# First feed-forward step of batches 1 to 7 fed from a transposed copy of x, with its LayerNorm applied behind the product

## The reference

```
x = x + 0.5 * ffn(layernorm(x))
x = x + attention(layernorm(x))          # 16 query heads, 4 key heads, head size 128,
                                         # rotary positions, causal window of 64
x = x + 0.5 * ffn(layernorm(x))
ffn(z) = (layernorm(z) * gamma + beta) @ ternary(weight).T + bias
```

## Time and profile before

| | us |
|---|---|
| median of 3 runs | 801.95 (799.03 to 803.97) |
| profiled execution, its own time | 804.61 |
| its span, first to last instruction | 802.8 |
| PE busy | 786.4 (98%) |
| DVE busy | 643.8 (80%) |
| ACT busy | 509.1 (63%) |
| POOL busy | 452.8 (56%) |

### The profile page before, as it was taken

One profiled execution on the slowest core, in us unless ns is written; L12 is line 12 of the kernel. 1 busy time (PEld: TensorE's weight loads), 2 busy tenths in 40 slices (PEclk: granted clock), 3 DMA queues, 4 the chain that ended last, 5 costly groups with the idle time before them and its releaser, 6 DMA issues. The chain is left out here.

```text
span 802.8 us, 16164 instructions
## 1 busy us (share of the span) xinstructions
PE 786.4 (98%) x5688; PEld 735.5 (92%) x5688; DVE 643.8 (80%) x1310; ACT 509.1 (63%) x1623; POOL 452.8 (56%) x440
## 2 busy tenths in 40 slices
PE   7899999999999999999999999999999999999997
PEld 6699999999999999999999999999999999999896
DVE  7788868978788887888779887797778888787666
ACT  4277665676656665676657766567665676665583
POOL 4767726575465645656545664456645574564533
PEclk9999999999999999999999999999999999999998
DMA  8462324341352423333233332434225341333500
GB/s 298 113 167 54 93 48 103 99 108 41 66 130 69 106 53 91 92 82 93 53 93 93 77 93 47 103 93 108 51 53 124 87 106 41 82 77 67 132 1 27
DMA packets 52447, 70.53 MB, mean 88 GB/s; under 512 B 7056, under 2 KB 30096, under 8 KB 52368
## 3 DMA queue, kind: packets, MB, share of 16 engines
q1 hardware_dynamic: 51808, 69.17, 35.4%
q10 hardware_dynamic: 560, 0.34, 0.1%
HBM read 10.76 MB, written 4.19 MB: 19 GB/s over the span
## 5 line engine op out<-in xcount | busy, mean ns | idle before, releaser
L1140 POOL TENSOR_TENSOR probs<-probs,inv_sum 128x512 f32<-128x512 f32 x128 | 133.2, 1041 | 186.6 <-DVE inv_sum L828 186.4
L1028 ACT ACTIVATE probs<-scores_p,neg_max 128x128 f32<-128x128 f32 x512 | 181.1, 373 | 50.7 <-DVE neg_max L822 50.2
L609 PE MATMUL attn_p<-wo_s,headsT 128*128 128x256 f32 x1536 | 209.8, 286 | 0.3 <-ACT headsT L1050 0.3
L609 PE MATMUL job_p<-xnT,wq_s 128*128 128x512 f32 x768 | 205.1, 403 | 0.8 <-DVE lnT L887 0.4
L609 PEld LDWEIGHTS attn_p<-wo_s,headsT 128*128 128x128 f32 x1536 | 197.1, 192 | 5.1 <-ACT headsT L1050 0.6
L1151 POOL TENSOR_TENSOR q_s<-q_s,rope_swap 128x512 f32<-128x512 f32 x128 | 164.7, 1294 | 52.1 <-DMA rope_swap<-rope_sin 51.8
L1050 ACT ACTIVATE headsT<-heads_p,columns_s 128x512 fp32r<-128x512 f32 x128 | 88.3, 690 | 146.7 <-PE heads_p L609 145.3
L609 PEld LDWEIGHTS job_p<-xnT,wq_s 128*128 128x128 f32 x768 | 136.0, 189 | 25.6 <-DVE k_s L867 1.1
L625 PE MATMUL scores_p<-k_s,q_s 128*128 128x128 f32 x1024 | 135.3, 275 | 2.0 <-POOL q_s L1151 2.0
L856 DVE SCALAR_TENSOR_TENSOR rope_sin<-job_p,columns_s,rope_t 128x512 f32<-128x512 f32 x160 | 119.1, 744 | 14.2 <-PE job_p L609 13.5
L625 PEld LDWEIGHTS scores_p<-k_s,q_s 128*128 128x128 f32 x1024 | 126.1, 192 | 3.9 <-POOL q_s L1151 2.2
(11 more groups left out here) (80 smaller groups left out, 974.1 us busy)
## 6 DMA issues: line engine op xcount, KB each, us to landing
rope_swap<-rope_sin SPq DMA_DIRECT2D x320, 128.0 KB, 2.3
v_odd<-v_s SPq DMA_DIRECT2D x64, 192.0 KB, 3.3
x_in<-x SPq DMA_DIRECT2D x15, 256.0 KB, 3.3
out<-x_res SPq DMA_DIRECT2D x15, 256.0 KB, 2.5
q_s<-wq SPq DMA_DIRECT2D x3, 512.0 KB, 10.2
q_s<-wo SPq DMA_DIRECT2D x2, 512.0 KB, 10.3
x_res<-wo SPq DMA_DIRECT2D x2, 512.0 KB, 4.2
x_res<-wv SPq DMA_DIRECT2D x1, 512.0 KB, 7.6
```

What stands on the lines that cost most here:

```text
L609: mm = nc.tensor.matmul(dst, a(p), b(q), start=clears and i == 0, stop=len(pairs) == 1, skip_group_check=True)
L1028: ins = nc.scalar.activation(probs[:, i, k, :], scores_p[i][:, k, :], ACT.Exp, bias=neg_max[:, i, k:k + 1], accum_out=row_sum[:, i, k:k + 1])
L1140: nc.gpsimd.tensor_tensor(probs[:, i, :, :], probs[:, i, :, :], inv_sum[:, i, :].unsqueeze(2).to_broadcast([P, 4, P]), ALU.mult).then_inc( ...
```

## The change

The host passes a second copy of x, transposed in each batch (x_transposed). For batches 1 to 7, load0 brings it into x_tr (512 KB, a third transfer behind the two of x_in), all on SP. YT no longer is a step of PE for these batches, and norm0/norm1 go from ACT: ACT and DVE make lnT straight from x_tr, without mean and rstd. FO multiplies as before. Behind it DVE computes rstd * product + x_in, one instruction of 128x256 for each block. What the mean contributes is -mean * rstd * (gamma summed through W), a row vector gamma_w: POOL's new step offset writes it for a half (128x512, over the part of x_tr that was read), and its new step center adds it to x_in; FO's addition waits for center. Gamma is halved once (gamma0i, POOL, first in its prologue, waits for the columns' transfer), so the factor 0.5 goes from FO's addition. gsum0i (PE, four matmuls, and a copy by DVE) makes gamma_w in the prologue. The mask is kept as two blocks and broadcast. Batch 0 and the second feed-forward steps keep their YT.

All tables are laid anew. What is spoken of below: load0n stands first in the middle list of SP, before the swap of K1c (it stood behind Q6c's); in the last list of SP, shift1c and store1p stand before Q10c, and store0p before K3c, where both stores stood between K3c, Q12c and Q14c; in the last list of TENSOR, FO0c stands behind O15c and YT2c (it stood before O15c); in its middle list, Q6c stands before T0c.

```diff
@@ TENSOR "middle"
-        K1c Q4c O13p W14p S0c T15p S1c Q5c V10c O14p W15p T0c Q6c S2c
...
-        W4c T5c YT0n S7c K3c O4c W5c T6c S8c Q12c YT1n O5c W6c Q13c
+        K1c O13p W14p Q4c S0c T15p S1c Q5c V10c O14p W15p Q6c T0c S2c
...
+        W4c T5c S7c K3c Q12c O4c W5c T6c S8c O5c Q13c W6c T7c S9c
@@ TENSOR "last"
-        T14c YT0c O13c W14c T15c O14c W15c FO0c O15c YT2c FO2c YT3c FO3c
+        YT0c T14c O13c W14c T15c O14c W15c O15c YT2c FO0c FO2c YT3c FO3c
@@ GPSIMD
-        scale0n scale1n half0i bias0n bias1n ascale0n ascale1n w6i w3i w1i w8i K0n Q0n Q1n
+        gamma0i scale0n scale1n half0i bias0n bias1n ascale0n ascale1n w6i w3i w1i w8i K0n Q0n
...
-        K1c Q4c probs0c scale0p probs1c Q5c bias0p Q6c probs2c scale1p Q7c K2c probs3c bias1p
-        Q8c probs4c scale0n probs5c Q9c Q10c probs6c bias0n scale1n Q11c bias1n K3c probs7c residual0c
+        K1c Q4c scale0p probs0c Q5c probs1c bias0p Q6c probs2c scale1p Q7c K2c probs3c bias1p
+        scale0n bias0n probs4c probs5c Q8c Q9c Q10c Q11c scale1n probs6c bias1n offset0n center0n probs7c
+        residual0c offset1n probs8c center1n ascale0n probs9c ascale1n K3c Q12c Q13c Q14c probs10c Q15c probs11c
@@ SYNC "middle" and "last"
-        K1c Q4c Q5c Q6c load0n Q7c K2c Q8c Q9c Q10c store0p store1p Q11c K3c
+        load0n K1c Q4c Q5c Q6c Q7c K2c Q8c Q9c Q10c shift1c Q11c store0p store1p
...
-        K1c Q4c Q5c Q6c Q7c K2c Q8c Q9c Q10c Q11c K3c shift1c store1p Q12c
-        Q13c store0p Q14c Q15c store2c store0c store3c
+        K1c Q4c Q5c Q6c Q7c K2c Q8c Q9c shift1c store1p Q10c Q11c store0p K3c
+        Q12c Q13c Q14c Q15c store2c store0c store3c
@@
+def from_x(x):
+    return x[0][-1] == "1" and x[2] > 0
...
+                sp.dma_start(x_tr[:, :, :], x_transposed[b].rearrange("(c p) t -> p c t", p=P)).then_inc(xt_loaded, 16)
...
+            def gamma_product(_):
+                for e in range(EC):
+                    mm = nc.tensor.matmul(attn_p[1][:, 0, :], gamma_s[:, e:e + 1].to_broadcast([P, P]),
+                                          w_tern[:, e, :].bitcast(F32), start=e == 0, stop=e == EC - 1)
...
@@ ffn_in_low (DVE, L887)
-                        out=lnT[:, r, 1, e, 0:width], in0=bank[:, e * width:(e + 1) * width],
+                        out=lnT[:, r, 1, e, 0:width], in0=transposed_part(x, e), scalar=gamma_s[:, e:e + 1], in1=lnT[:, r, 0, e, 0:width].bitcast(F32), op0=ALU.mult,
...
@@ ffn_out (DVE, L902), for batches 1 to 7
+                        ins = nc.vector.scalar_tensor_tensor(out=dst[:, at, :], in0=bank[:, k, :], scalar=rstd[:, at:at + 1],
+                                                             in1=src[:, at, :], op0=ALU.mult, op1=ALU.add)
...
@@ POOL
+            def mean_offset(x):
+                nc.gpsimd.tensor_tensor(scratch_of(m), gamma_w[:, :].unsqueeze(1).to_broadcast([P, 2, E]),
+                                        shift[:, half].unsqueeze(2).to_broadcast([P, 2, E]),
+                                        ALU.mult).then_inc(offset_ready, 1)
+            def center(x):
+                nc.gpsimd.tensor_tensor(x_in[:, half, :], x_in[:, half, :], scratch_of(m), ALU.add).then_inc(centered, 1)
+            def halve_gamma(_):
+                pool.wait_ge(columns_in, 16)
+                nc.gpsimd.tensor_scalar(gamma_s, gamma_s, 0.5, None, ALU.mult).then_inc(gamma_ready, 1)
```

More of the change, by code:

```diff
@@ L59 @@
     "prologue": """
-        fill0i total0i fill1i YT0n YT1n fill2i beta0i FO0n fill3i FO1n open0i fill4i XT0n fill5i
-        XT1n V00n K0n Q0n Q1n Q2n Q3n V01n
+        fill0i total0i fill1i YT0n YT1n fill2i beta0i FO0n fill3i FO1n open0i gsum0i fill4i XT0n
+        fill5i XT1n V00n K0n Q0n Q1n Q2n Q3n V01n
     """,
     "first": """
-        K1c Q4c Q5c S0c S1c Q6c V10c T0c Q7c S2c W0c T1c S3c K2c
-        O0c W1c T2c Q8c S4c Q9c V11c O1c W2c T3c Q10c O2c W3c S5c
-        T4c S6c Q11c O3c W4c T5c YT0n S7c K3c O4c W5c Q12c O5c T6c
@@ L67 @@
[L67 to L70, removed]
+        K1c Q4c Q5c S0c S1c Q6c V10c T0c S2c Q7c W0c T1c K2c O0c
+        S3c Q8c W1c T2c Q9c V11c S4c O1c W2c T3c Q10c O2c W3c S5c
+        T4c S6c O3c Q11c W4c T5c S7c O4c W5c T6c K3c Q12c O5c FO0n
+        W6c S8c Q13c T7c O6c S9c Q14c W7c FO1n Q15c T8c XT0n O7c W8c
@@ L80 @@
+        T12c Q2n S14c O11c Q3n W12c V01n T13c S15c O12c W13c T14c
     """,
     "last": """
[L82 to L85, removed]
+        K1c O13p Q4c S0c W14p T15p S1c Q5c O14p W15p V10c Q6c T0c S2c
+        Q7c O15p W0c T1c S3c YT0p K2c O0c W1c Q8c YT1p T2c S4c Q9c
@@ L86 @@
+        O1c FO0p W2c Q10c T3c V11c O2c S5c Q11c W3c FO1p T4c S6c O3c
+        W4c K3c Q12c T5c S7c Q13c O4c W5c Q14c Q15c T6c S8c O5c W6c
         T7c S9c O6c W7c T8c S10c O7c W8c T9c S11c O8c W9c T10c S12c
         O9c W10c T11c S13c O10c W11c T12c S14c O11c W12c T13c S15c O12c W13c
-        T14c YT0c O13c W14c T15c O14c W15c FO0c O15c YT2c FO2c YT3c FO3c
+        YT0c T14c O13c W14c T15c O14c W15c O15c YT2c FO0c FO2c YT3c FO3c
     """,
@@ L103 @@
[L103 to L106, removed]
+        K1c Q4c Q5c max0c max1c inv0c Q6c inv1c w11f probsT0c max2c V10c Q7c heads0c
+        inv2c K2c probsT1c max3c Q8c heads1c inv3c Q9c probsT2c max4c stats0n heads2c inv4c probsT3c
@@ L107 @@
+        V11c Q10c max5c heads3c max6c inv5c stats1n probsT4c Q11c inv6c heads4c probsT5c max7c YT0n
+        w12f K3c heads5c probsT6c YT1n inv7c Q12c FO0n heads6c astats0n max8c probsT7c Q13c max9c
+        Q14c inv8c FO1n astats1n heads7c probsT8c inv9c Q15c max10c heads8c XT0n probsT9c XT1n inv10c
+        max11c K0n heads9c inv11c probsT10c max12c Q0n heads10c inv12c probsT11c max13c V00n heads11c Q1n
+        inv13c probsT12c Q2n max14c heads12c max15c inv14c Q3n probsT13c inv15c V01n
     """,
@@ L108 @@
     "middle": """
[L109 to L113, removed]
@@ L117 @@
+        inv5c V11c heads3c FO1p Q11c probsT4c stats1n max6c max7c inv6c probsT5c heads4c K3c heads5c
+        Q12c inv7c probsT6c max8c YT1n Q13c heads6c inv8c FO0n probsT7c max9c astats0n Q14c FO1n
+        inv9c astats1n heads7c probsT8c Q15c max10c heads8c probsT9c XT0n max11c XT1n inv10c K0n heads9c
+        probsT10c inv11c heads10c max12c Q0n inv12c probsT11c V00n max13c Q1n heads11c inv13c probsT12c max14c
+        Q2n inv14c Q3n heads12c max15c probsT13c inv15c V01n
     """,
     "last": """
-        probsT14p heads13p K1c Q4c evac0p max0c heads14p stats0p max1c probsT15p Q5c inv0c V10c Q6c
@@ L120 @@
[L120 to L124, removed]
@@ L125 @@
-        evac0c stats0c heads12c max15c inv14c probsT13c norm0c heads13c inv15c probsT14c YT0c evac1c heads14c probsT15c
-        stats2c heads15c FO0c norm2c evac2c stats3c YT2c norm3c FO2c YT3c FO3c
+        heads13p K1c evac0p probsT14p Q4c max0c heads14p max1c stats0p probsT15p Q5c inv0c V10c Q6c
+        inv1c max2c heads15p probsT0c Q7c evac1p stats1p probsT1c heads0c inv2c max3c YT0p K2c Q8c
+        heads1c probsT2c inv3c YT1p Q9c max4c FO0p inv4c heads2c Q10c probsT3c V11c max5c inv5c
+        Q11c heads3c probsT4c max6c FO1p K3c heads4c inv6c max7c probsT5c Q12c inv7c Q13c heads5c
@@ L127 @@
+        Q14c Q15c max8c probsT6c heads6c inv8c probsT7c max9c heads7c inv9c max10c probsT8c inv10c heads8c
+        max11c probsT9c heads9c inv11c max12c probsT10c inv12c heads10c max13c probsT11c inv13c heads11c max14c probsT12c
+        evac0c stats0c heads12c max15c inv14c probsT13c norm0c inv15c heads13c probsT14c evac1c YT0c heads14c probsT15c
+        stats2c heads15c norm2c evac2c stats3c FO0c YT2c norm3c FO2c YT3c FO3c
     """,
@@ L137 @@
     "first": """
[L138 to L142, removed]
@@ L195 @@
     "first": """
-        load0n K1c Q4c Q5c Q6c Q7c K2c stage9f Q8c Q9c Q10c Q11c K3c Q12c
-        Q13c shift1c Q14c Q15c K0n Q0n Q1n Q2n Q3n shift0n
+        K1c load0n Q4c Q5c Q6c Q7c K2c Q8c Q9c stage9f Q10c shift1c Q11c K3c
+        Q12c Q13c Q14c Q15c K0n Q0n Q1n Q2n Q3n shift0n
     """,
     "middle": """
-        K1c Q4c Q5c Q6c load0n Q7c K2c Q8c Q9c Q10c store0p store1p Q11c K3c
-        shift1c Q12c Q13c Q14c Q15c K0n Q0n Q1n Q2n Q3n shift0n
+        load0n K1c Q4c Q5c Q6c Q7c K2c Q8c Q9c Q10c shift1c Q11c store0p store1p
+        K3c Q12c Q13c Q14c Q15c K0n Q0n Q1n Q2n Q3n shift0n
     """,
     "last": """
-        K1c Q4c Q5c Q6c Q7c K2c Q8c Q9c Q10c Q11c K3c shift1c store1p Q12c
-        Q13c store0p Q14c Q15c store2c store0c store3c
+        K1c Q4c Q5c Q6c Q7c K2c Q8c Q9c shift1c store1p Q10c Q11c store0p K3c
+        Q12c Q13c Q14c Q15c store2c store0c store3c
     """,
@@ L255 @@
 BIASED = {part: numbered(POOL_STEPS, "bias" + part) for part in "123"}
+OFFSETS = numbered(POOL_STEPS, "offset")
+CENTERED = numbered(POOL_STEPS, "center")
 LOW_DVE = numbered(DVE_STEPS, "w")
@@ L286, in blocks_of, with block_kernel @@
     return slice(first, first + block_count(x))
-def block_kernel(nc, x, wq, wk, wv, wo, ffn_wT, columns, rows, rope_tables, mask, ident, out):
+def block_kernel(nc, x, x_transposed, wq, wk, wv, wo, ffn_wT, columns, rows, rope_tables, mask, ident, out):
```

(7 more changed lines are left out.)

165 lines of the change are left out of this document (107 added, 58 removed).

## The result

| | us |
|---|---|
| before, median (4 runs beside the changed kernel) | 802.16 (799.03 to 803.97) |
| changed, median of 4 runs | 833.75 (828.84 to 836.81) |
| ratio, 95% interval | 1.039 (1.033 to 1.045) |
| span of the profiled execution, before and after | 802.8 and 834.7 |

What follows compares the result with a forecast made beforehand. The prediction took PE, busy for 94.91 of 95.00 us in a middle batch, as the bound. Its terms, -6.2 + 1.4 + 1.5 - 0.4 - 2.0 - 0.4 + 2.2 = -3.9 us, gave 798.0 us, range 791 to 806.

Steps and rivals of the forecast that it cites:

- PE work that goes: Seven batches lose two YT steps of PE each, 14 x 0.44 us, all on the path: -6.2 us.
- Where a batch begins: Loads ahead of K1c's swap make T0c late by 0.25 us in each of six batches: +1.5 us.
- the loads take the gain: Rival: K1c's swap lands late, T0c waits 1 us or more in six batches; 802.5 us, chance 0.15.
- outer bound, 20 us: Upper bound for the wait where a middle batch begins: 3.3 us of loads times six batches.
- The port: POOL holds up DVE's low part of lnT, now with two SBUF inputs: 0.1 us for 14 halves, +1.4 us.
- POOL's new steps are covered: Offset and center, 5.2 us a batch on POOL, leave probs6c to probs8c in time for T6 to T8: 0.
- Charging all 28 instructions alike: Half of 1.29 us on each low-part instruction of lnT, 18 us of DVE's time; not used in the sum.
- T0 of two batches: The 0.2 us that T0 starts late in two batches goes with the new order: -0.4 us.
- The last batch: The scores' wait for Q15c shrinks by about 1 us, the clock's loss perhaps spared: -2.0 us, bounds 0 and -3.7.
- the end: FO0c moves into a gap behind YT2c, so the closing chain starts earlier: -0.4 us, bounds -0.95 and +0.3.
- The prologue: gamma0i at the head of POOL's list waits for the columns and delays rstd: +2.2 us, bounds 0 and 2.9.

Runs made afterwards that it cites:

- e4: The kernel before with three of four transposes left out of each YT step of the first FFN, batches 1 to 7: 796.79 us, ratio 0.993.
- e9: The changed kernel with load0n behind Q6c, gamma0i behind scale1n, and DVE's YT1n behind Q13c and heads6c: 797.78 us, ratio 0.995.
- e1: The changed kernel with load0n moved back behind Q6c in SP's middle list: 808.35 us, ratio 1.008.
- e8: The kernel before with its load0n (512 KB) moved to the head of SP's middle list: 806.48 us, ratio 1.003.
- e6: The changed kernel with load0n behind Q6c, POOL's offset1n before residual0c, and gamma0i behind scale0n and scale1n: 800.73 us, ratio 0.996.
- e10: The changed kernel with load0n behind Q6c and gamma0i behind scale1n in POOL's prologue: 805.77 us, ratio 1.004.
- e7: The changed kernel with the x_tr transfer issued by ACT behind probsT14p instead of by SP: 826.26 us, ratio 1.027.
- e3: The changed kernel with POOL's offset1n moved before residual0c in the middle list: 830.47 us, ratio 1.034.

## Why the prediction was wrong

**PE work that goes, -6.2: right.** e4 gives 5.7 us (4.2 to 7.3 by its interval) for three quarters of it; its six middle batches are 3.7 us shorter for 36 transposes, 0.10 us each, where the prediction had 0.11. In e9 the six middle batches are 6.4 us shorter than before; 48 transposes at 0.11 are 5.3 of it.

**Where a batch begins, +1.5: the step that failed, 29.8 us of span by e1 (25.4 by the medians).** The mechanism was named, and the rival "the loads take the gain" had it as the whole story, but at 1 us a batch. The prediction put T0's due time 13.7 us behind K1 and needed some 4.5 us on POOL behind the landing; measured 13.6 and 4.5. The landing was wrong: forecast 9.7 us behind K1's start, measured 12.6. I had priced 1 MB at 318 GB/s, the best stretch, added it to the old landing and left everything else in place. Without the loads the swap lands at 7.7 in the new order (e1) instead of 6.45, and the loads cost 4.9 us instead of 3.3, of which the time that SP takes to issue them, 2.0 us, was put at nothing. Half of the difference between 6.45 and 7.7 is the choice of the row: batch 4, from which I read 6.45, is among the two earliest of the six, which lie at 6.4 to 8.2 with a mean of 7.05. That turns a lateness of 0.5 us into 3.4 (17.0 us from K1 to T0 in the mean, against 13.6), 20 us over six batches. I then halved the 0.5 for an overlap that no row showed, near a threshold past which every further microsecond is paid in full. The other 9.5 us follow from the clock: from the third middle batch on, T0 to S5 takes 1.6 to 2.8 us more than 19.7. The prediction had the clock's fall behind a wait in its own rows, for the last batch, and did not apply it to the wait that it was pricing. The medians give less than the spans because both the waits and the clock's fall differ from run to run (828.84 to 836.81 us). The prediction's outer bound, 20 us, was for the waits alone, and was not taken into the range.

**The port, +1.4: right mechanism, mis-sized, 7.6 us.** The price per meeting was taken from a POOL instruction of 1.29 us and the meetings as evenly spread. What counts is which instruction meets which: in an order written by hand the same pair meets in each batch, here YT1n and the residual addition of 2.37 us. The first half's pair never mattered. The claim that POOL's new steps are covered held: no T6 to T8 waits. The Trainium skill's rule ("SBUF — State Buffer", "Who interferes with whom": a DVE instruction with two SBUF inputs contends with a GpSimd instruction that reads SBUF, one with at most one SBUF input outside the 2-port modes does not) agrees with the two L921 rows above, 0.482 and 2.656 us at most. Of the rows that the prediction put beside the rule for two inputs, only the subtraction in the prologue (0.426 and 1.01 us) bears on it; the instruction on two columns at 419.28 has a single tensor as its input. Charging all 28 instructions alike, as the prediction tried beside its sum, has the size wrong: the median stays at 0.480, and one instruction in each middle batch carries the cost.

**T0 of two batches, -0.4:** swallowed by the above. **The last batch, -2.0, and the end, -0.4: not shown.** The two profiles have -1.7 in both together: the wait shrank by 0.55 us, not by 1, and the clock was spared, the upper end of that term. But where the clock held, the lists of the kernel before were as quick: K1 of the last batch to PE's end is 98.7 us in e4 and 99.4 in e8 (with a wait of 2.27 us), and 98.9 to 99.3 in all runs with the new lists. So the -1.7 is of the size of what the clock's fall cost in the one profiled execution before, no run shows a gain of the new order, and that the number comes near the forecast is luck. The end's share was not measured by itself.

**The prologue, +2.2: right**, +2.0, with rstd at 8.65 (forecast near 9.0); e6 and e10 confirm the cause. The size varies with the clock: K1 of batch 0 starts at 34.1 to 35.1 us with the old prologue, at 36.6 to 38.7 with gamma0i first, and at 33.5 to 34.3 with gamma0i behind scale1n. Batch 0, +0.8, was not in the sum, though 0.9 of the -6.2 should have come there; which of its new waits makes up the difference was not tried.

The terms as measured, from span to span: -6.4 (before to e9, middle batches), +7.6 (e9 to e10) and +29.8 (e10 or e1 to the changed kernel) are the +31.0 of the middle batches; with +2.0, +0.8 and -1.7 that makes 32.1, and the span grew by 31.9. The same by the medians: -4.5 for e9 against the kernel before, +8.0 for the port, +2.6 for gamma0i, +25.4 for the loads, 31.5 in all, and the medians differ by 31.6. Both chains close by construction; what they give is the size of each step.

## What to carry to other kernels

When a transfer is placed in front of others that an engine waits for, price it at the mean rate of a full moment with all that is under way then, add the time to issue it, take the landing from all repetitions and not from one, and compare it with the room left. Here each microsecond beyond the room was paid in each batch, and waits of some 2 us and more at times cost PE its clock on top. Moving an operand from PSUM to SBUF can make a DVE instruction meet POOL's: look in the order for the pair that meets each time, and move one of the two. A step at the head of an engine's list that waits for a late transfer delays the whole list.

## What the runs showed of the hardware that was not expected

- One DVE instruction of 0.48 us took 2.64 us when it started 0.01 us behind a POOL addition of 2.37 us; moved 2.3 us behind that addition's start, with Q13 and heads6 before it, the pair took 0.87 us.
- The transfers around a batch's start ran at 219 GB/s over 3 us in the changed kernel, with swaps, x_tr and the end of x_in under way:

```profile
434.00:437.00 3.00, 3.00 (x26) 2.96 (x25) 2.55 (x5) 0.88 (x3) 0.00 (x0) 1.00 0.89 219
```

- x_tr on another queue, landed before the swap went out, still cost most of the loss, by way of the loads behind it: 826 against 834 us.
- PE's granted clock fell to 0.50 at a wait of 3.3 us, and not at 1.44 us in the last batch. Between these the length of the wait alone did not decide: it fell at waits of 1.99 us (kernel before), 2.03 and 2.40 us (e7), and held at 2.23 and 2.76 us (changed kernel), 2.27 us (e8) and 2.91 us (e3). e7's 2.03 us first, then e3's 2.91 us, each with the stretch behind it:

```profile
536.69 0.66 PE L706 MATMUL probsT_p<-identf,probs 128*128 128x128 f32 x4 [2.03 <-POOL probs L1202]
...
538.00:541.00 3.00, 3.00 (x10) 2.42 (x10) 2.01 (x4) 3.00 (x15) 0.86 (x1) 0.50 0.00 0
...
541.59 0.65 PE L707 MATMUL probsT_p<-identf,probs 128*128 128x128 f32 x4 [2.91 <-POOL probs L1198]
...
543.00:546.00 3.00, 3.00 (x22) 2.74 (x21) 2.82 (x6) 3.00 (x14) 1.31 (x2) 1.00 0.00 0
```
